# Low-rank attention: 64-row product pairs, key scores chained by differences of key tiles, one block of full products a head

## The reference, cut to what matters

```python
c_q = h @ W_DQ + b_DQ                      # 32 columns
c_kv = h @ W_DKV + b_DKV                   # 32 columns
q_c = (c_q @ W_UQ + b_UQ);  k_c = (c_kv @ W_UK + b_UK);  v_c = (c_kv @ W_UV + b_UV)
q_r = (c_q @ W_QR + b_QR);  k_r = (h @ W_KR + b_KR)      # 32 columns a head, k_r shared
scores = (q_c @ k_c.T + q_r @ k_r.T) / sqrt(128 + 32)
out = softmax(scores) @ v_c                # 1024 x 1024 scores a head
h + concat_heads(out) @ W_O + b_O
```

## Time and profile before

| | |
|---|---|
| median of 3 runs | 1808.41 us (1804.92 to 1810.31) |
| span of the profiled execution | 1812.5 us (the page gives no other time of that execution) |
| PE busy | 1670.4 us, 92% of the span |
| PE weight loads (PEld) | 1223.0 us, 67% |
| DVE busy | 1393.8 us, 77% |
| ACT busy | 1137.5 us, 63% |
| POOL busy | 1177.3 us, 65% |
| first row product, first key product, last key product | 584.2, 610.8, 1778.0 us |

### The profile page before, as it was taken

One profiled execution on the slowest core, in us unless ns is written; L12 is line 12 of the kernel. 1 busy time (PEld: TensorE's weight loads), 2 busy tenths in 40 slices (PEclk: granted clock), 3 DMA queues, 4 the chain that ended last, 5 costly groups with the idle time before them and its releaser, 6 DMA issues.

```text
span 1812.5 us, 39662 instructions
## 1 busy us (share of the span) xinstructions
PE 1670.4 (92%) x15057; PEld 1223.0 (67%) x15057; DVE 1393.8 (77%) x2976; ACT 1137.5 (63%) x2222; POOL 1177.3 (65%) x909
## 2 busy tenths in 40 slices
PE   4679999999877899999999999999999999999995
PEld 4557777777766567666766766766676677677674
DVE  5557777766597888878888888888887888888862
ACT  5447777777676466666666666666656666665662
POOL 4300111000066498898898988989889898898892
PEclk9889999999887899999999999999999999999997
DMA  4556666654000000000000000001001000100101
GB/s 123 136 140 156 162 156 159 164 136 116 29 1 1 1 10 8 10 8 10 7 13 16 10 8 19 11 7 22 7 10 19 8 10 7 22 7 10 19 10 30
DMA packets 198677, 81.47 MB, mean 45 GB/s; under 512 B 152553, under 2 KB 177493, under 8 KB 198357
## 3 DMA queue, kind: packets, MB, share of 16 engines
q1 hardware_dynamic: 198484, 78.93, 19.5%
HBM read 39.79 MB, written 29.88 MB: 38 GB/s over the span
## 4 chain that ended last, share of the span: by engine, by line
PE 54%; DVE 11%; POOL 2%; issue 1%; ACT 1%; DMA 0%; SPq 0%; POOLq 0%; ACTq 0%
PE pair L1825 12%; PE pair L1878 11%; PE pair L1882 11%; PE pair L1936 10%; DVE amax L1833 4%; PE pair L1929 4%; PE pair L1650 2%; DVE o_inv L1946 1%; PE pair L1641 1%; DVE stats L485 1%; POOL w_mix L1907 1%; PE pair L1664 1%; DVE q_low L1754 1%; DVE cq L1765 1%; DVE key_hl L1768 1%
## 5 line engine op out<-in xcount | busy, mean ns | idle before, releaser
L1893 ACT ACTIVATE prob<-pair 128x512 f32<-128x512 f32 x1024 | 604.4, 597 | 422.2 <-PE pair L1882 359.6
L1833 DVE TENSOR_REDUCE amax<-pair 128x1 f32<-128x512 f32 x1024 | 670.3, 682 | 133.9 <-PE pair L1825 131.8
L1825 PE MATMUL pair<-key_hl,q_hi 128*128 128x512 f32 x1024 | 437.8, 430 | 11.2 <-DVE amax L1833 7.1
L1878 PE MATMUL pair<-q_hi,key_hl 128*128 128x512 f32 x1024 | 405.2, 396 | 2.6 <-ACT prob L1893 2.6
L1882 PE MATMUL pair<-q_low,key_h 65*128 65x512 f32 x1024 | 406.0, 396 | 0.0
L1907 POOL TENSOR_TENSOR w_mix<-w_mix,prob 128x1024 f32<-128x1024 f32 x160 | 382.3, 2389 | 25.2 <-ACT prob L1893 8.5
L1907 POOL TENSOR_TENSOR Wm<-Wm,prob 128x1024 f32<-128x1024 f32 x155 | 369.6, 2384 | 20.8 <-ACT prob L1893 4.1
L520 POOL TENSOR_SCALAR veps<-mv 128x8 f32<-128x8 f32 x47 | 11.4, 243 | 452.6 <-DVE mv L493 451.2
L1825 PEld LDWEIGHTS pair<-key_hl,q_hi 128*128 128x128 f32 x1024 | 196.1, 192 | 115.9 <-issue 51.0
L1936 PE MATMUL pair<-prob,values 128*32 128x256 f32 x4096 | 247.2, 382 | 0.0
L1186 DVE TENSOR_REDUCE mx_neg<-pair 128x4 f32<-128x512 f32 x256 | 164.9, 687 | 94.8 <-PE pair L1090 94.1
(11 more groups left out here) (209 smaller groups left out, 2232.8 us busy)
## 6 DMA issues: line engine op xcount, KB each, us to landing
rows_mem<-once SPq DMA_DIRECT2D x128, 128.0 KB, 2.0
queries<-rows_mem SPq DMA_DIRECT2D x64, 256.0 KB, 4.5
keys<-rows_mem SPq DMA_DIRECT2D x16, 1024.0 KB, 7.1
rows_mem<-once SPq DMA_DIRECT2D x128, 64.0 KB, 1.9
q_low<-shift_cols SPq DMA_DIRECT2D x512, 0.5 KB, 2.0
yT<-o_norm SPq DMA_DIRECT2D x256, 32.0 KB, 1.9
x<-x_dram SPq DMA_DIRECT2D x8, 512.0 KB, 7.3
out_dram<-x SPq DMA_DIRECT2D x7, 512.0 KB, 3.4
```

Source lines behind the costliest of these rows:

```text
L1825: e.matmul(row_bank(("row", r, i)), q_hi[:, k, t * P:(t + 1) * P], key_hl[:, b % 2, i * HALF:(i + 1) * HALF], start=True, stop=True, skip_ ...
L1833: e.tensor_reduce(amax1[:, u % 2, t, i:i + 1], row_bank(("row", r, i)), AX_X, ALU.max).then_inc(*row_maxed.up((r, i)))
L1878: e.matmul(bank(j), key_hl[:, b % 2, ks], q_hi[:, k, sl], start=True, stop=False, skip_group_check=True)
L1893: e.activation(prob1[:, g % P_BUFS, half * HALF:(half + 1) * HALF], bank(K_BANKS[(2 * g + half) % 3]), ACT.Exp, scale=SCALE1).then_inc(*ke ...
```

## The change

- **Layout.** `q_hi` and `q_low` hold queries 0 to 511 in rows 0 to 63 and 512 to 1023 in rows 64 to 127, `[P, 3, 512]`. One query product of two accumulated matmuls, with zeros around the weights, fills both halves. Keys are in both halves too (`key_high`, `key_low`), copied or computed twice.
- **Pairs.** Row and key products contract over 64 rows, and are issued in pairs, one for each half of the rows, into the two banks of a `pair`. A row pair covers 2 x 128 queries against 512 keys; its score is `q_hi` with `key_high` alone. One maximum a pair, 128 x 2 from 128 x 2 x 512, and one top a head.
- **Chained key scores.** Tiles 0 and 1 of a head are four terms: high x high, low x high, high x low, and ones x shift (`q_shift`, eight DMAs a head, one buffer). Tiles 2 to 7 are three terms with `start=False`: differences of the key tile to the one two before, `step_high` and its rest in `key_low`, added onto the scores that stand in the same pair of banks since step g - 2.
- **Differences.** New items a batch: GpSimd subtracts features two tiles apart (`y_step`, 128 x 768), TensorE multiplies them with the key weights ("diff": for each half of 384 columns two products into rows 0 to 63 and 64 to 127), ScalarE and VectorE split the result.
- **Banks.** Key pairs use pairs 0 and 1; row pairs, the query, the weighing block and items take pairs 2 and 3 in turn (`use`, `pair_free`): each may start when the use two before it has been read.
- **One block a head.** At step g % 8 = 3 no row pair is issued (the next step has two), and the query, the whole weighing of the head before and one pair of items stand there. The totals read tiles 6 and 7 and `key_sum`, which GpSimd makes in five sums.
- **Exponentials** are one instruction a tile, 128 x 1024; `prob` is a ring of 12 tiles.
- **Values** come from the features in fp32 (two instructions each) with `value_bias` added by VectorE.
- **Norm work** of the last layer is one entry a head (`NORM_WORK`) on the head's block step.

```diff
-ROW_LEAD = 14
-Q_BUFS, P_BUFS = 3, 8
+ROW_LEAD = 13
+QUERY_LEAD = 13
+BURST = 3
+Q_BUFS, P_BUFS = 3, 12
+ROW_PAIRS = 2, 3
+SUMMED = 6
...
+def rows_at(g):
+    r = g + ROW_LEAD
+    return {BURST: [], BURST + 1: [r - 1, r]}.get(g % NT, [r])
...
+    def use(key, held):
+        places[key] = ROW_PAIRS[len(uses) % 2], uses[-2] if len(uses) >= 2 else None
+        uses.append(held)
+
+    def items_at(b, h):
+        kind, a = {0: ("quant", b - 2), 1: ("proj", b - 1), 2: ("product", b - 2), 3: ("turn", b + 1),
+                   4: ("low", b + 1), 5: ("diff", b + 1), 6: ("value", b + 1)}.get(h, (None, 0))
...
             if kind == "query":
-                e.matmul(bank(j), w_query[:, h, :], cq[:, b % 2, sl], start=True, stop=True,
+                e.matmul(bank(j), w_query[:, h, KR:3 * KR], cq[:, b % 2, 0:HALF], start=True, stop=False,
+                         skip_group_check=True)
+                e.matmul(bank(j), w_query[:, h, 0:2 * KR], cq[:, b % 2, HALF:T], start=False, stop=True,
...
+            elif kind == "diff":
+                e.wait_ge(*y_stepped.at(a))
+                for side in range(2):
+                    ins = e.matmul(bank(j)[side * KR:(side + 1) * KR, 0:3 * P], w_low[:, 0:KR],
+                                   y_step[:, i * 3 * P:(i + 1) * 3 * P], start=True, stop=True, skip_group_check=True)
...
-            row_bank_free(e, ("row", r, i))
-            e.matmul(row_bank(("row", r, i)), q_hi[:, k, t * P:(t + 1) * P], key_hl[:, b % 2, i * HALF:(i + 1) * HALF],
-                     start=True, stop=True, skip_group_check=True).then_inc(*row_scored.up((r, i)))
+            pair_free(e, ("row", r))
+            for side in range(2):
+                rows = slice(side * KR, (side + 1) * KR)
+                ins = e.matmul(bank(2 * places_m["row", r][0] + side), q_hi[rows, k, t * P:(t + 1) * P],
+                               key_high[rows, b % 2, half * HALF:(half + 1) * HALF], start=True, stop=True,
+                               skip_group_check=True).then_inc(*row_scored.up((r, side)))
...
-            e.tensor_reduce(amax1[:, u % 2, t, i:i + 1], row_bank(("row", r, i)), AX_X, ALU.max).then_inc(
-                *row_maxed.up((r, i)))
+            e.tensor_reduce(amax1[:, u % 2].rearrange("p (s t) k -> p s t k", s=2)[:, :, t, half],
+                            pair[places_m["row", r][0]][:, :].rearrange("p (s n) -> p s n", s=2), AX_X,
+                            ALU.max).then_inc(*row_maxed.up(r))
...
-            if n >= 3:
-                e.wait_ge(*key_exp.at(divmod(n - 3, 2)))
-            e.matmul(bank(j), key_hl[:, b % 2, ks], q_hi[:, k, sl], start=True, stop=False, skip_group_check=True)
...
-            e.matmul(bank(j), key_h1[:, b % 2, ks], q_low[:, k, sl], start=False, stop=True,
-                     skip_group_check=True).then_inc(*key_scored.up((g, half)))
+            if g >= 2:
+                e.wait_ge(*key_exp.at(g - 2))
+            if t < 2:
+                terms = (key_high[:, b % 2, ks], q_hi), (key_low[:, b % 2, ks], q_hi), \
+                    (key_high[:, b % 2, ks], q_low), (ones_shift[:, :], q_shift)
+            else:
+                steps = step_high[:, b % 2, (t - 2) * P:(t - 1) * P]
+                terms = (steps, q_hi), (key_low[:, b % 2, ks], q_hi), (steps, q_low)
+            for part, (weights, moving) in enumerate(terms):
...
+                for side in range(2):
+                    rows = slice(side * KR, (side + 1) * KR)
+                    n = 0 if moving is q_shift else k
+                    ins = e.matmul(banks[side], weights[rows, :], moving[rows, n, :], start=t < 2 and part == 0,
+                                   stop=part == len(terms) - 1, skip_group_check=True)
...
+            e.activation(prob1[:, g % P_BUFS, :], pair[g % 2][:, :], ACT.Exp, scale=SCALE1).then_inc(*key_exp.up(g))
...
+            weighed, totals = weigh_banks(u)
+            pair_free(e, ("weigh", u))
+            e.wait_ge(*value_ready.at(b))
+            e.wait_ge(*key_exp.at(NT * u + NT - 1))
+            tiles = [prob1[:, (NT * u + t) % P_BUFS, :] for t in range(NT)]
+            parts = tiles
+            if u < B * NH - 1:
+                e.wait_ge(*summed_keys.at(NT * u + SUMMED - 1))
+                parts = *tiles[SUMMED:], key_sum[u % 2]
...
         def pe_low_rank(e):
...
+                if 0 <= g < total:
+                    pe_key_scores(e, g)
+                for r in rows:
+                    pe_row_scores(e, r)
+                if query is not None:
+                    pair_free(e, ("query", query))
+                    pe_low_part(e, ("query", query, 0), 2 * places_m["query", query][0])
+                if weigh is not None:
+                    pe_weigh(e, weigh)
+                if items:
+                    pair_free(e, ("items", g))
+                for n, item in enumerate(items):
+                    pe_low_part(e, item, 2 * places_m["items", g][0] + n)
```

More of the change, by code:

```diff
@@ L247, in prepare @@
-    def prepare(b):
-        return ([(kind, b, i) for kind in ("turn", "low") for i in range(2)]
-                + [("const", b, 0), ("value", b, 0)])
-    def regular(g):
-        for i in range(2):
-            u, rest = divmod(g + 16 - 4 * i, NT)
-            if rest == 0 and 0 <= u < U:
-                return "query", u, i
-        return None
-    opening = {"bias": [((("bias", 0, 0), None, None), 1)]}
-    for item, j in zip(prepare(0), (2, 3, 4, 5, 2, 3)):
-        run = begin(item, j)
-        opening.setdefault(item[0], []).extend((tuple(run[:3]), part) for part in range(1, PARTS[item[0]] + 1))
@@ L1359, in pe_layers @@
                 elif i == B - 1:
-                    for (item, j, before), part in opening_m["turn"]:
-                        pe_low_part(e, item, j, before, part)
+                    pe_opening(e, "turn")
                 if i == 0:
@@ L1372, in pe_layers @@
                 elif i == B - 1:
-                    for (item, j, before), part in opening_m["low"]:
-                        pe_low_part(e, item, j, before, part)
+                    pe_opening(e, "low")
                 if i < 2:
@@ L1420, in dve_layers @@
                 if i == B:
-                    for (item, j, before), part in opening_m["low"]:
-                        dve_low_part(e, item, j, before, part)
+                    dve_opening(e, "low")
                 if i >= 1:
@@ L1859, in sync_move_shift @@
[L1859 to L1868 removed]
+                e.wait_ge(*shift_ready(u - 1))
@@ L1993, in pe_low_rank @@
             e.wait_ge(*x_dve.at(("c", B - 2)))
-            for g, early, late in plan_m:
+            e.wait_ge(*keys_done.at((0, 1)))
+            for g, features, copies, final, rows, work, query, weigh, items in plan_m:
                 if g == CONST_AT:
-                    for kind in ("const", "value"):
-                        for (item, j, before), part in opening_m[kind]:
-                            pe_low_part(e, item, j, before, part)
+                    pe_opening(e, "value")
                 elif g == LAST_C["turn"]:
@@ new lines, in dve_low_rank @@
+                for part, half in final:
+                    dve_final(e, part, half)
+                for r in rows:
+                    dve_row_max(e, r)
+                    if r % NT == NT - 1:
+                        dve_row_top(e, r // NT)
+                if query is not None:
+                    dve_low_part(e, ("query", query, 0), 2 * places_m["query", query][0])
+                for kind, b in work:
+                    dve_norm_work(e, kind, b)
+                if weigh is not None:
+                    dve_invert_totals(e, weigh)
+                    dve_normalise(e, weigh)
@@ new lines, in dve_low_rank @@
+                for n, item in enumerate(items):
+                    dve_low_part(e, item, 2 * places_m["items", g][0] + n)
+        def pool_low_rank(e):
+            work_before = []
+            for g, features, copies, final, rows, work, query, weigh, items in plan_m:
+                for item in features:
+                    pool_low_after(e, item)
+                for part, half in final:
+                    pool_final(e, part, half)
+                r = g + ROW_LEAD - SHIFT_LAG
+                if r % NT == 0 and 0 <= r - NT < total:
+                    pool_shift(e, r // NT - 1)
+                for kind, b in work_before:
+                    pool_norm_work(e, kind, b)
+                work_before = work
+                if (g - 1) % NT in range(1, SUMMED) and 0 <= g - 1 < total - NT:
```

623 lines of the change are left out of this document (312 added, 311 removed).

## The result

Four runs of the changed kernel took 1758.22 to 1762.12 us, median 1761.26, beside a median of 1808.2 for the kernel before: a ratio of 0.9732 (0.9715 to 0.9748), 47 us less. The forecast was 1727, with 1761 inside its range. Direction and mechanism came out; 34 us of the forecast gain did not.

What follows compares the result with a forecast made beforehand. TensorE was taken as the bound, others close. With 15.4 us a head, a batch takes 138.2; seven batches -75, the last -10, tail +2, opening +2: together -81 us, so 1727 us, range 1694 to 1795.

Steps and rivals of the forecast that it cites:

- Block and maxima in series: New loop: the block starts only after the head's last row maximum, so both add up; 15.4 us a head.
- The two-bank maximum: VectorE's row maximum over two banks of 512: 1.14 us each, bounds 1.08 and 1.36; eight take 9.1.
- Rival 1: Two-bank maxima cost more than one and a half; at 1.36 us the kernel takes 1840; chance 0.06.
- Pairs: Key and row products on TensorE: two 64-row halves run together, 0.237 us a pair, 34 pairs a head 8.1.
- rival 4: Halves of a pair run in series on TensorE: 21.4 us a head, about 2100 us; chance 0.03.
- Rival 3: Weight loads not hidden in TensorE's pairs: 0.32 to 0.35 us a pair, 1785 to 1810 us; chance 0.05.
- rival 2: TensorE's clock falls to the low level for half of the stretches: +128, 1855 us; chance 0.05.
- Side products: TensorE's short products behind the block, before the next row product: 15.0 us a batch, all in the loop.
- Last batch: Last eight heads of the stage: 125.3 us against 135.0 before, -10.
- Neither ends last: ScalarE's exponentials and GpSimd's sums don't set the head; both would if it came below some 14.3 us.
- The sentence on short cover: VectorE's other steps hide under the 4.8 us block; where short, the next row product's arrival, 1.2 us later, covers them.
- The opening's +2: Opening: ScalarE copies before the last transposes of the stage ahead cost +2 us, between 0 and 5.

Runs made afterwards that it cites:

- experiments 4: Changed kernel with each row pair read by two maxima over 512 columns instead of one over 1024; 1780.65 us.
- 7: Changed kernel with a head's first row pair issued right behind the block and its short products, ahead of the next key tile; 1736.83 us.
- 3: Changed kernel with a head's first row pair issued inside the weighing block and its maximum run during the block; 1789.54 us.
- experiment 5: Changed kernel with the last of the three key terms added twice in key tiles 2 to 7, one more pair each; 1774.24 us.
- Experiment 6: Changed kernel with both halves of every key and row pair reading rows 0 to 63; measured once, 2307.14 us.
- experiment 9: Changed kernel with GpSimd's feature difference behind the sums, first row pair before the key tile, query and last row pair earlier; 1823.88 us.
- Experiment 1: Changed kernel with GpSimd's difference of the features moved behind that head's five sums; 1745.49 us.

## Why the forecast was right, and where it failed

- **Block and maxima in series**, 15.4 a head: measured 15.40. By experiments 4 and 7 the row of maxima is the path; by the chains of 3 and 5 TensorE follows closely.
- **The two-bank maximum** at 1.14 when queued: 9.14 for eight with 1.22 for the last. Rival 1 fell.
- **Pairs** at 0.237: 0.233. Experiment 6 gives rival 4 its price, 21.5 a light head by measurement and 21.4 by the forecast. Rival 3 fell too: the statement of the Trainium skill, "TensorE: Matmul & The Clock Gate", Part 3, The mechanism, that a load overlaps only where the row groups differ, does not hold here; pairs that follow each other in the same rows start 0.23 apart. A pair may cost 0.30, the forecast said: experiment 5 put five pairs into most steps instead of four, 1.16 us for the 1.14 there are, and lost 0.36 a head, 0.33 of it outside the maxima. So the 0.30 was too generous: the forecast's own sum has three key pairs between block and first maximum, and a longer pair adds there at once.
- **The block** at 4.8: 4.58 to its last product, 4.9 to the next key product. Exponentials took 1.025 from PSUM, not 0.92; nothing hung on it.
- **The clock**, rival 2, did not fall for whole stretches, and in light heads not at all: 11 stretches, 38 us, most behind GpSimd's wait or the values' short products, not behind the waits for banks that the forecast had named for it (and the Trainium skill, same page, "A second HAM failure mode: psum-queue depth-cycling"). Such falls came in experiment 9, where TensorE waited up to 2.9 us for a place. At the lower level pairs started 0.42 apart (606.04 and 606.46), near the 0.43 taken.
- **Side products** 15.0: 13.9. **Last batch** 125.3: 126.5 (from 1594.08 to 1720.57), and the seven before it 988.0 instead of 957: the time is missing in the seven.
- **The step that failed** is "Neither ends last", and with it "The new subtraction of features on GpSimd (some 1.8 us) runs beside it". The load was right, 114 of 138 us forecast and 112.4 of 143.4 measured. But the order was not read: in its queue the subtraction waits 3.4 us for ScalarE, three of the head's five sums (7.4 us) have to pass behind it, and the block waits for the last. Experiment 1 puts the price at 22 us of the 32 that the stage lacks.
- **The sentence on short cover** ("the next row product's arrival covers it") held for the scales of the quantisation, but VectorE's parts of the low-rank item, which wait for ScalarE's four copies, were not in it: 1.5 a batch, 10 us. This was read from the trace and not isolated by a run.
- The opening's +2 can't be judged: it varies by more from one execution to the next.

## What to carry to other kernels

When an engine is judged free because its load fits, walk its queue once in order: one instruction that waits for another engine moves everything behind it, and what counts is when the last of them ends, not the sum. When work is made serial on purpose, ask of each piece between the two parts whether it may stand under either of them; moving one row pair 0.7 us forward gained at least as much as the fused maximum (25.8 against 14.4 us of the stage, up to 24 without the help that the clock gave there). And before an instruction is moved, see what stands behind it on every queue that it passes: the two edits here that freed a place early each lost more than they gained.

## What the runs showed of the hardware

- Two 64-row products of 512 columns in different halves of the rows start 3 to 4 ns apart in most cases and take the time of one (0.233); in the same rows they take 0.465.
- In experiment 6 TensorE was granted the lower clock for stretches of 24 to 58 us, 398 of 1649 us, and through the one shown it was busy without a gap. They began behind a wait of 0.8 to 0.9 us (seven) or behind short products (six). In the other kernels a fall in the steady batches lasted 3 to 7 us and stood behind idle time or short products where it was looked at. Why it stayed low so long here is open.
- Whether the clock falls behind the same wait changes from kernel to kernel: after 2.4 us of waiting the block took 6.26 us in five of six batches of the changed kernel (5.97 in the sixth); after 2.0 and 2.2 in experiments 4 and 5 it took 6.2 to 6.3 in two of six each, and 4.58 in the other four.
- Column-tiled products of 32 columns and 64-row products don't mix freely: a single pair inside the block cost 0.34 beside its own 0.23.
